# A two-layer fusion block on one core: the last stage's kept norm two images ahead, its sums one image ahead, and the constants loaded after the first image

## The chip, the cores and the metric

The kernel runs on one core of a Trainium2 chip. The metric is the device time of one execution in microseconds (us). Times of events are us from the start of the profiled span. PE is TensorE, DVE is VectorE, ACT is ScalarE, POOL is GpSimd, and SP is SyncE, which here only issues DMAs.

## What is computed

32 images are cut into 196 patches each and projected to 128 columns; 77 text rows are put behind them, so an image has 273 rows. Then come an attention block with mixed heads and a mixture of experts, each added to its input. The tail of the reference is what the last stage computes:

```
h = h + _L0_attn_ref(_layernorm(h, axis=-1), ...)
h = h + _L0_ffn_ref(_layernorm(h, axis=-1), ...)

def _L0_ffn_ref(x, ...):
    xn = layer_norm(x, ln_g, ln_b)
    logits = jnp.einsum('bsd,de->bse', xn, Wg)
    ...                                        # top 2 of 8 experts, two matrices each
    combined = jnp.einsum('bskd,bsk->bsd', sel, conf)
    return layer_norm(x + combined, out_g, out_b)
```

So for each image the end is: y = norm(h), t = y + (the two chosen experts' results), out = h + norm(t) * out_g + out_b.

## The kernel before

There are three stages. The attention stage goes image by image, with nine turns (one for each of eight heads, and one for the last rows) per image, and overlaps three images. It writes h of each image to DRAM (`h1`), keeps the mean and scale of the second norm in SBUF (`kept`), and scatters the normalised rows to the experts' regions in DRAM. The expert stage takes 76 tiles of 256 rows, and scatters the weighted results back to DRAM, two choices for each row. The final stage goes through the 32 images once more. There is no scheduler: the order on each engine is the order in which the code is written.

**How the final stage is ordered.** `slots(eng, total, stages, ring)` walks through steps s on one engine. `stages` is a list of pairs (a, function); in step s the functions run in the listed order, each for image s + a. So a = 2 means that an engine does this part two steps before the image's own step. Each engine has its own list, and engines meet only through semaphores. Of every buffer there are eight, one for each image modulo 8 (`UE`); of the PSUM banks there are four for each of two uses. The parts of image k are:

- SP, `load_image` (six steps ahead): three DMAs, the two expert results (two DMAs, lines 416 and 418) and h (line 419, into a part of `w1hl`); from image 8 on they wait for the output of image k - 8. `store` (two steps behind): two DMAs, lines 423 and 425.
- ACT, `normed3` (line 839): y from h with the kept scale and bias, three activations of 98x128, into `Y3` (a part of `w2s`, so that profile rows call it `w2s`). It waits for the load (`in`) and for a copy of the kept values (`nr3`).
- PE, `sums` (line 1450): the two experts' results are added by two matmuls with the identity. It waits for the load and for the PSUM bank of image k - 4 (`t3`).
- DVE, `sum3` (line 1163): t = sums + y, into `T3` (profile rows call it `w1hl`). Then `stats3`: bn_stats (line 876, three), a small copy (879), bn_aggr (881, three) into `mv3`.
- POOL, `norm3` (lines 651 to 656): four tiny operations that make scale and bias of the third norm.
- ACT, `scale3` (line 847): t times scale plus bias, three activations, in place. It waits for POOL's last one.
- DVE, `scale3` (line 1173): times out_g, in place, both operands in SBUF. It waits for ACT's `scale3`.
- PE, `kept_rows` (line 1458): h + out_b in PSUM; it waits for the output of image k - 4 (`fin`).
- DVE, `output` (line 1182): the sum, into `fin` (profile rows call it `VP`).

DVE also copies the kept values (`stats_back`, line 1156). On DVE the order in step s is stats_back, scale3 of image s - 2, sum3 of s, output of s - 2, stats3 of s.

**How the kernel starts.** SP issues in turn the token weights `wtok` (384 KB), image 0 (588 KB), its text rows (38.5 KB), `wqkv` (320 KB), `cosT` (294 KB), image 1 (588 KB) and its text rows. ACT issues at the same time the bias of the experts (4 KB, line 662) and `small` (1297 KB, line 663), which holds all small constants; it then waits for image 0 (`x0`) and issues the experts' weights (lines 666 to 668, 4 MB). PE's token matmuls of image 0 (line 1201) wait for `wtok` and image 0. DVE waits for `small` before four short preparations (lines 867 to 871), and then adds the token bias, which lies in `small`, to PE's result (line 890).

Of the kernel before, what the change touches and what calls it, by code (L numbers as in the profile page):

```python
# [25 lines left out]
B, C, IMG, P16 = 32, 3, 224, 16  # L26
# [31 lines left out]
UE = 8  # L58
# [28 lines left out]
def early_fusion_kernel(nc, x, txt, w_tok, w_qkvr, small_in, w1, b2, w2, rope, tail, tiota,  # L87
# [5 lines left out]
    with ctx:  # L93
# [3 lines left out]
        def sem(name):  # L97
            return ctx.enter_context(nc.semaphore(name))
# [156 lines left out]
        S = {n: sem(n) for n in names.split()}  # L255
# [46 lines left out]
        def slots(eng, total, stages, by_expert=(), ring=UP):  # L302

            ahead = [a for a, _ in stages]

            def expert(t):
                return eng.value_load(tab[0:1, 0, bass.ds(t, 1)], min_val=0, max_val=NE - 1)

            def peeled(s):
                for a, stage_ in stages:
                    if 0 <= s + a < total:
                        stage_(s + a, (s + a) % ring, *([expert(s + a)] if stage_ in by_expert else []))
            for s in range(-max(ahead), 2 * ring):
                peeled(s)


            halves = []
            for h in range(2):  # L320
                need = {u + a for a, stage_ in stages if stage_ in by_expert for u in (2 * h, 2 * h + 1)}
                if need:
                    first, count = min(need), max(need) - min(need) + 1
                    regs = [eng.alloc_register(f"expert{h}{n}") for n in range(count)]
                    halves.append((first, regs, {first + n: bass.RuntimeValue.of_register_unchecked(
                        r, min_val=0, max_val=NE - 1) for n, r in enumerate(regs)}))

            def load_experts(h, s):
                if halves:
                    first, regs, _ = halves[h]  # L330
                    eng.reg_load(regs, tab[0:1, 0, bass.ds(s + first, len(regs))])
            load_experts(0, 2 * ring)
            with eng.Fori(2 * ring, total - 2 * ring + 1, ring) as s:
                for u in range(ring):
                    if u == 0:
                        load_experts(1, s)
                    if u == 2:
                        load_experts(0, s + ring)
                    for a, stage_ in stages:
                        stage_(s + (u + a), (u + a) % ring,  # L340
                               *([halves[u // 2][2][u + a]] if stage_ in by_expert else []))
            for s in range(total - ring, total - min(ahead)):
                peeled(s)
# [3 lines left out]
        def _(sp):  # L347
# [22 lines left out]
            def step(i, par, has):  # L370
# [6 lines left out]
                if has["load"]:  # L377
# [4 lines left out]
            sp.wait_ge(S["w2_loaded"], 48)  # L382
            sp.wait_ge(S["ends_ready"], 1)
            _, ends = nc.values_load_multi_w_load_instructions(basu[0:1, :], engines=[sp.engine], min_val=0,
                                                               max_val=DUMMY - TT)
            for row in [*ends, DUMMY]:
# [273 lines left out]
        @block.scalar  # L660
        def _(act):
            act.dma_start(bias[:], b2).then_inc(S["bias_in"], 16)
            act.dma_start(small[:], small_in).then_inc(S["small_weights"], 16)
            act.wait_ge(S["x0"], 16)
            for a in range(2):
                act.dma_start(stage[:, a, :], w1[:, a * 2048:(a + 1) * 2048]).then_inc(S["w1_loaded"], 16)
            for dst, src in ((w2s, w2), (tio, tiota), (tailt, tail)):
# [175 lines left out]
            def scale3(k, p):  # L843
# [3 lines left out]
                    last = nc.scalar.activation(T3[p][:, t], T3[p][:, t], ACT.Identity, bias=nm3[:, p, t:t + 1],  # L847
                                                scale=rs3[:, p, t:t + 1])
                last.then_inc(S["c3"], 1)
            slots(act, B, [(0, normed3), (-1, scale3)], ring=UE)  # L850


        @block.vector
        def _(dve):
# [321 lines left out]
            def output(k, p):  # L1176

                dve.wait_ge(S["res_ps"], k + 1)
                if not below(k, UE):
# [1 line left out]
                dve.wait_ge(S["g3"], k + 1)  # L1181
                v.tensor_tensor(fin[p], T3[p], PS[0:R, 4 + p % 4, 0:w].rearrange("p (t d) -> p t d", t=NT), ALU.add
                                ).then_inc(S["fin"], 1)
            slots(dve, B, [(3, stats_back), (-2, scale3), (0, sum3), (-2, output), (0, stats3)], ring=UE)


        @block.tensor
        def _(pe):
# [264 lines left out]
            def kept_rows(k, p):  # L1453
                if below(k, 1):
                    pe.wait_ge(S["bias_row"], 16 * UE)
                if not below(k, 4):
                    pe.wait_ge(S["fin"], k - 3)
                mm(PS[0:R, 4 + p % 4, 0:w].rearrange("p (t d) -> p t d", t=NT), sumb[:], H3b[p], start=True, stop=True
                   ).then_inc(S["res_ps"], 1)
            slots(pe, B, [(0, sums), (-1, kept_rows)], ring=UE)  # L1460


# [83 lines left out]
```

## Time and profile before

| | |
|---|---|
| median of 3 runs | 1436.22 us (1434.65 to 1436.59) |
| the profiled execution's own time | 1437.18 us |
| its span | 1435.3 us |
| PE busy / ACT / DVE / POOL | 92% / 71% / 62% / 58% of the span |
| attention stage | to about 1035 us |
| expert stage | about 1035 to 1315 us |
| final stage, first load issued / first sum / end | 1320.5 / 1327.5 / 1435.3 us |

How to read it: over the whole span PE is the busiest engine, but the figure is a mean over stages. In the final stage no engine is busy all the time, and the last stage is about 8% of the span. There, the chain of waits (which work released which, followed back from the end) says more than busy shares. A row of the timeline shows start, duration, engine, line, operation, output and inputs, how many were merged, and in brackets the idle time before it with what ended it.

### The profile page before, as it was taken

To read this page: it belongs to the slowest core of one execution; us is meant where nothing else is said; L and a number is where in the kernel's file an instruction comes from. 1 tells how busy PE (TensorE), PEld (TensorE's weight loads), DVE (VectorE), ACT (ScalarE), POOL (GpSimd) and SP (SyncE) were. 2 spreads that over 40 slices of the span, in tenths; PEclk is the share of its full clock that TensorE was granted. 3 is DMA by queue.
4 is the path that set the end of the run, shared out by engine and by line. 5 is a ranking of instruction groups with operands and counts; after the bars stand their busy time and mean duration, and the time that the engine had idled before them with its cause. 6 is when DMAs were issued, how large, how long until landed. Compare 5 with 4: busy or idle time off the path is not lost.

```text
span 1435.3 us, 34511 instructions
## 1 busy us (share of the span) xinstructions
PE 1317.1 (92%) x8386; PEld 1099.1 (77%) x8387; DVE 894.0 (62%) x3124; ACT 1024.7 (71%) x3008; POOL 837.9 (58%) x1845
## 2 busy tenths in 40 slices
PE   5899999999999999999999999997699999997874
PEld 4777788777887777787778877776599999996331
DVE  3776666776666766667666667664355444443777
ACT  2688887888888888878888888887155555553676
POOL 2136665566665566655666655666556666665444
PEclk9999999999999999999999999999599999998987
DMA  6001111111110101110111101100222222222763
GB/s 238 19 28 32 37 51 35 31 35 31 50 38 31 35 31 34 50 35 31 35 31 50 38 31 35 31 15 28 72 70 78 77 77 77 75 73 61 198 178 95
DMA packets 69507, 82.39 MB, mean 57 GB/s; under 512 B 11650, under 2 KB 59773, under 8 KB 68946
## 3 DMA queue, kind: packets, MB, share of 16 engines
q1 hardware_dynamic: 57264, 57.17, 13.6%
q0 software_dynamic: 11328, 19.07, 4.3%
q10 hardware_dynamic: 866, 5.60, 0.9%
q8 instruction: 18, 0.29, 0.1%
q14 instruction: 31, 0.25, 0.1%
HBM read 52.13 MB, written 30.65 MB: 58 GB/s over the span
## 4 chain that ended last, share of the span: by engine, by line
PE 55%; DVE 18%; POOL 10%; issue 9%; ACT 5%; DMA 1%; DVEq 1%; ACTq 0%; POOLq 0%; SPq 0%
PE PS L1285 10%; PE PS L1438 10%; PE PS L1247 8%; PE PS L1201 6%; PE PS L1265 4%; DVE bst L876 4%; DVE nmax L954 3%; PE PS L1425 3%; PE PS L1427 3%; PE PS L1426 3%; PE PS L1291 2%; POOL rs L466 2%; ACT E L696 2%; DVE xn L901 2%; POOL qT L489 2%
## 5 line engine op out<-in xcount | busy, mean ns | idle before, releaser
L1247 PE MATMUL PS<-kT,qs 128*128 128x273 f32 x1024 | 281.8, 398 | 1.8 <-ACT E L696 1.4
L1285 PE MATMUL PS<-AT,VP 128*128 128x273 f32 x1024 | 279.4, 395 | 0.0
L696 ACT ACTIVATE E<-PS,nmax 128x273 f32<-128x273 f32 x512 | 243.9, 484 | 25.7 <-DVE nmax L954 21.1
L954 DVE TENSOR_REDUCE nmax<-PS 128x2 f32<-128x546 f32 (+1 forms) x288 | 206.8, 718 | 72.3 <-PE PS L1247 72.3
L585 POOL DMA_INDIRECT dram_routed<-xr,slu x192 | 189.0, 984 | 60.5 <-issue 60.5
L1247 PEld LDWEIGHTS PS<-kT,qs 128*128 128x128 f32 x1024 | 184.4, 190 | 36.2 <-issue 2.9
L641 POOL DMA_INDIRECT dram_results<-arena,du x152 | 166.0, 1092 | 62.9 <-issue 53.3
L723 ACT COPY AT<-PS 128x512 f32<-128x512 f32 x256 | 150.1, 586 | 60.7 <-PE PS L1265 60.7
L1285 PEld LDWEIGHTS PS<-AT,VP 128*128 128x128 f32 x1024 | 175.5, 191 | 20.6
L1265 PEld LDWEIGHTS PS<-small,E 128*128 128x128 f32 x1024 | 126.2, 141 | 53.1 <-ACT ATR L730 22.0
L1265 PE MATMUL PS<-small,E 128*128 128x128 f32 x1024 | 156.4, 274 | 8.9 <-ACT ATR L730 8.7
L1438 PE MATMUL PS<-w2s,VP 128*128 x1216 | 156.3, 278 | 0.0
L1438 PEld LDWEIGHTS PS<-w2s,VP 128*128 128x128 f32 x1216 | 148.4, 192 | 0.0
L679 ACT ACTIVATE qs<-qT,small 128x256 f32<-128x256 f32 x256 | 128.5, 503 | 24.3 <-POOL qT L489 24.3
L933 DVE RECIPROCAL rsum<-esum 128x2 f32<-128x2 f32 (+1 forms) x288 | 45.4, 157 | 160.0 <-ACT E L696 143.0
L826 ACT ACTIVATE VP<-PS,b1f 128x256 f32<-128x256 f32 x304 | 119.3, 474 | 31.8 <-PE PS L1427 31.8
L709 ACT ACTIVATE E<-E,rsum 128x256 f32<-128x256 f32 x256 | 132.7, 518 | 8.7 <-DVE rsum L933 5.0
L505 POOL TENSOR_TENSOR EK<-E,rsum 128x34 f32<-128x34 f32 x256 | 63.1, 253 | 90.9 <-DVE rsum L933 89.0
L817 ACT CAST rounded<-PS 128x256 fp32r<-128x256 f32 x76 | 28.3, 372 | 119.5 <-PE PS L1413 119.5
L939 DVE TENSOR_SCALAR E<-E,rsum 128x256 f32<-128x256 f32 x256 | 101.7, 397 | 9.0
L1201 PE MATMUL PS<-wtok,arena 128*98 128x128 f32 x768 | 98.6, 280 | 9.2 <-DMA arena<-in_x 9.0
L696 ACT ACTIVATION_READ_ACCUMULATOR E<-PS,nmax 128x1 f32 x512 | 102.7, 200 | 0.0
(191 smaller groups left out, 2790.4 us busy)
## 6 DMA issues: line engine op xcount, KB each, us to landing
arena<-in_x SPq DMA_DIRECT2D x32, 588.0 KB
arena<-dram_routed SPq DMA_DIRECT2D x76, 144.0 KB
dram_h<-H SPq DMA_DIRECT2D x32, 147.0 KB
w1hl<-dram_h SPq DMA_DIRECT2D x32, 147.0 KB
stage<-dram_results SPq DMA_DIRECT2D x16, 196.0 KB
AT<-dram_results SPq DMA_DIRECT2D x16, 196.0 KB
out<-VP SPq DMA_DIRECT2D x32, 98.0 KB
dram_routed<-xr,slu POOLq DMA_INDIRECT x192, 2.3
```

The costliest lines, as they stand in the source:

```text
L585: g_.indirect_dma_start(out=routed, out_offset=bass.IndirectOffsetOnAxis(ap=slu[0:rows, par, k, t:t + 1], axis=0), in_=xr[0:rows, par, t, ...
L641: g_.indirect_dma_start(out=results.rearrange("n (k d) -> (n k) d", k=2), out_offset=bass.IndirectOffsetOnAxis(ap=du[:, u, h, :], axis=0), ...
L679: nc.scalar.activation(qs[:, g % QR, :], qT[:, par, 0:MQ], ACT.Copy, scale=wpre[:, g:g + 1]).then_inc(S["q_scaled"], 1)
L696: nc.scalar.activation(bank, PS[0:rows, 2 * ((par + u) % 2) + t, 0:N], ACT.Exp, bias=nmax[0:rows, u, t:t + 1], accum_out=esum[0:rows, u, t ...
L709: last = nc.scalar.activation(own_tile, own_tile, ACT.Copy, scale=rsum[:, u, 1:2])
L723: nc.scalar.copy(AT[:, u - 1, :, 0:MQ], PS[:, TB, :].rearrange("p (c q) -> p c q", c=FULL)).then_inc(S["probsT_sb"], 1)
L954: v.tensor_reduce(nmax[0:rows, u], PS[0:rows, b0:b0 + 2, 0:N], AX.X, ALU.max, negate=True).then_inc(S["max"], 1)
L1201: last = mm(PS[0:R, MA, t * D:(t + 1) * D], xt[:, p, q, t * R:(t + 1) * R], wtok[:, q, :], start=(q == 0), stop=(q == QP - 1))
L1247: last = mm(PS[0:rows, 2 * ((par + u) % 2) + t, 0:N], q, kT[:, par, 0:N], start=True, stop=True)
L1265: last = tr(PS[:, TB, at:at + 128], E[:, (u - 1) % EB, t, keys], idn[:])
L1285: last = mm(acc, VP[:, par, g, c, :], AT[:, g, c, :], start=(g == 0 and c == 0), stop=False)
L1438: mm(o, GT[:, u % 2, c, h * 128:(h + 1) * 128], w2s[:, bass.ds(e * FH + c * D, D)], start=(c == 0), stop=False)
```

## The change

Three numbers and the place of one wait differ. In the final stage ACT's `normed3` runs two images ahead instead of in the image's own step, and PE's `sums` one image ahead. The copy of the kept values, which `normed3` needs, goes from three to four ahead on DVE. At the start ACT's wait for image 0 stands ahead of the DMA of `small` instead of behind it.

```diff
@@ -660,8 +660,8 @@
             act.dma_start(bias[:], b2).then_inc(S["bias_in"], 16)
+            act.wait_ge(S["x0"], 16)
             act.dma_start(small[:], small_in).then_inc(S["small_weights"], 16)
-            act.wait_ge(S["x0"], 16)
             for a in range(2):
@@ -847,7 +847,7 @@
-            slots(act, B, [(0, normed3), (-1, scale3)], ring=UE)
+            slots(act, B, [(2, normed3), (-1, scale3)], ring=UE)
@@ -1181,7 +1181,7 @@
-            slots(dve, B, [(3, stats_back), (-2, scale3), (0, sum3), (-2, output), (0, stats3)], ring=UE)
+            slots(dve, B, [(4, stats_back), (-2, scale3), (0, sum3), (-2, output), (0, stats3)], ring=UE)
@@ -1457,7 +1457,7 @@
-            slots(pe, B, [(0, sums), (-1, kept_rows)], ring=UE)
+            slots(pe, B, [(1, sums), (-1, kept_rows)], ring=UE)
```

What stands in a row on ACT at the start of the kernel, before; names are destination and source, and brackets show what an instruction waits for.

```order
L662 DMA bias<-in_b 128x8
L663 DMA small<-in_small 128x2594
L666 DMA stage<-in_w 128x2048 [waits x0]
L666 DMA stage<-in_w 128x2048
L668 DMA w2s<-in_w 128x4096
```

After the change ACT has there:

```order
L662 DMA bias<-in_b 128x8
L664 DMA small<-in_small 128x2594 [waits x0]
L666 DMA stage<-in_w 128x2048 x2
L668 DMA w2s<-in_w 128x4096
L668 DMA tio<-in_tiota 1x152
```

The wait for image 0 moved from the first expert weights to `small`, which stands ahead of them.

ACT at the start of the final stage (L839 is `normed3`, L847 `scale3`, three activations for an image), as one piece of the difference:

```order
 L826 ISA
 L826 ACTIVATE VP<-PS,b1f 128x256
-L839 ACTIVATE w2s<-w1hl,nr 98x128 x6
+L839 ACTIVATE w2s<-w1hl,nr 98x128 x12
 L847 ACTIVATE w1hl<-w1hl,nm,rs 98x128 x3
 L839 ACTIVATE w2s<-w1hl,nr 98x128 x3
```

Ahead of the first `scale3` there were two images of `normed3`, and now there are four; from there on the two alternate as before, and at the end four images of `scale3` stand in a row instead of two.

PE at the start of the final stage, before (L1450 is `sums`, two matmuls for an image, L1458 `kept_rows`):

```order
L1440 MATMUL PS<-b2hl,ones 128x128
L1450 MATMUL PS<-stage,small 98x384 x4
L1458 MATMUL PS<-w1hl,small 98x384
L1450 MATMUL PS<-stage,small 98x384 x2
L1458 MATMUL PS<-w1hl,small 98x384
L1450 MATMUL PS<-stage,small 98x384 x2
```

After the change PE has there:

```order
L1440 MATMUL PS<-b2hl,ones 128x128
L1450 MATMUL PS<-stage,small 98x384 x6
L1458 MATMUL PS<-w1hl,small 98x384
L1450 MATMUL PS<-stage,small 98x384 x2
L1458 MATMUL PS<-w1hl,small 98x384
L1450 MATMUL PS<-AT,small 98x384 x2
```

The first `kept_rows` stood behind the sums of two images, and now stands behind those of three.

## Rows read from the trace of the kernel before

**Rows 1.** Windows, final stage: length, PE, PEld, DVE, ACT, POOL busy, clock, DMA, GB/s.

```profile
1332.00:1420.00 88.00, 67.77 (x175) 29.54 (x173) 67.82 (x297) 65.03 (x166) 41.00 (x107) 0.92 0.61 171
```

**Rows 2.** Chain of waits, one turn of the final stage: start, us, what.

```profile
1363.35 0.04 ACT w1hl L847
...
1364.61 1.17 ACT w2s L839 x3
...
1365.87 0.09 DVE w1hl L1163
...
1367.66 0.23 DVE mv L881 x3
...
1367.96 0.49 POOL nm L651
...
1369.84 0.05 ACT w1hl L847
```

**Rows 3.** Timeline of the same stretch: start, us, engine, line.

```profile
1361.36 0.55 DVE L1173 TENSOR_TENSOR w1hl<-w1hl,small 98x384 f32<-98x384 f32 x1
1361.47 0.49 POOL L651 TENSOR_TENSOR nm<-mv,mone 98x3 f32<-98x3 f32 x1 [2.50 <-DVE mv L881]
...
1363.35 1.26 ACT L847 ACTIVATE w1hl<-w1hl,nm,rs 98x128 f32<-98x128 f32 x3 [1.77 <-POOL nm L656]
...
1363.53 0.30 DVE L881 BATCH_NORM_AGGREGATE mv<-bst 98x2 f32<-98x6 f32 x3
...
1363.92 0.20 POOL L651 TENSOR_TENSOR nm<-mv,mone 98x3 f32<-98x3 f32 x1 [0.60 <-DVE mv L881]
...
1364.64 0.56 DVE L1173 TENSOR_TENSOR w1hl<-w1hl,small 98x384 f32<-98x384 f32 x1 [0.75 <-ACT w1hl L847]
...
1365.67 1.25 ACT L847 ACTIVATE w1hl<-w1hl,nm,rs 98x128 f32<-98x128 f32 x3
```

**Rows 4.** Timeline, DVE's line 1173 for images 0, 28 and 31.

```profile
1332.19 0.56 DVE L1173 TENSOR_TENSOR w1hl<-w1hl,small 98x384 f32<-98x384 f32 x1 [0.78 <-ACT w1hl L847]
...
1422.97 0.56 DVE L1173 TENSOR_TENSOR w1hl<-w1hl,small 98x384 f32<-98x384 f32 x1 [0.80 <-ACT w1hl L847]
...
1431.54 0.56 DVE L1173 TENSOR_TENSOR w1hl<-w1hl,small 98x384 f32<-98x384 f32 x1 [0.90 <-ACT w1hl L847]
```

**Rows 5.** Timeline of ACT, and one stretch of the windows, as the final stage begins.

```profile
1327.00 1.26 ACT L839 ACTIVATE w2s<-w1hl,nr 98x128 f32<-98x128 f32 x3 [1.11 <-DMA w1hl<-dram_h]
1330.89 0.88 ACT L847 ACTIVATE w1hl<-w1hl,nm,rs 98x128 f32<-98x128 f32 x2 [2.63 <-POOL nm L656]
...
1326.00:1332.00 6.00, 6.00 (x15) 2.85 (x14) 3.34 (x18) 2.37 (x6) 1.93 (x7) 0.74 0.95 248
```

**Rows 6.** Timeline of PE's line 1458 for two images running, and that stretch's window.

```profile
1373.43 1.58 PE L1458 MATMUL PS<-w1hl,small 99*98 99x384 f32 x2 [1.86 <-DVE VP L1182]
...
1377.37 1.48 PE L1458 MATMUL PS<-w1hl,small 99*98 99x384 f32 x2
...
1374.00:1378.00 4.00, 4.00 (x7) 1.71 (x6) 3.21 (x17) 2.24 (x7) 2.72 (x7) 0.50 0.73 192
```

**Rows 7.** Timeline and windows, start of the kernel.

```profile
8.78 0.27 DVE L867 CAST trb<-small 98x196 bf16<-98x196 f32 x1 [5.09 <-DMA small<-in_small]
...
9.23 0.17 DVE L871 COPY base<-small 98x8 f32<-98x8 f32 x1
14.51 0.42 DVE L890 TENSOR_TENSOR H<-PS,small 98x256 f32<-98x256 f32 x1 [5.12 <-PE PS L1201]
...
9.03 5.44 PE L1201 MATMUL PS<-wtok,arena 128*98 128x128 f32 x24 [9.03 <-DMA arena<-in_x]
...
2.00:5.00 3.00, 0.00 (x0) 0.00 (x0) 0.34 (x2) 0.00 (x0) 1.99 (x7) 1.00 0.93 368
5.00:9.00 4.00, 0.00 (x0) 0.00 (x0) 0.22 (x2) 0.00 (x0) 0.36 (x1) 1.00 1.03 390
9.00:12.00 3.00, 2.97 (x14) 2.97 (x15) 0.36 (x4) 0.70 (x1) 0.05 (x1) 1.00 1.10 408
```

## The prediction

> **What bounds the kernel now.** I read three views in turn. First the windows, to see whether an engine is full in the stage that the change touches. From 1332 to 1420 us DVE is busy for 67.8 of 88 us, ACT for 65.0, PE for 67.8, and the DMA engines move 171 GB/s at a share of 0.61 [rows 1]: nobody is full, so a chain of waits sets the pace. Then the chain of waits there. It repeats with a period of 1369.84 - 1363.35 = 6.49 us [rows 2], and one turn does two images: on DVE, line 1173 of image 0 starts at 1332.19 and of image 28 at 1422.97, 90.78 us for 28 images, 3.24 us each [rows 4]. One turn is ACT's `scale3`, then ACT's `normed3` of a later image, then DVE's line 1163, which waits for that `normed3`, then output and statistics, POOL's norm, and ACT again. So y, which depends on nothing in the loop, sits in it because ACT takes its work in the order in which it is written. Third the timeline of the start: PE's first matmul waits until 9.03 us for image 0, and `small`, which has landed by 8.78 us, is needed by nobody on the path before line 890 at 14.51 us [rows 7].
>
> **The final stage, term by term.** The present turn, from the rows: from ACT's line 847 to the start of DVE's line 1163, 1365.87 - 1363.35 = 2.52 us; from there to the end of the last bn_aggr, 1367.66 + 0.23 - 1365.87 = 2.02; from there through POOL to ACT's next line 847, 1369.84 - 1367.89 = 1.95. Sum 6.49 [rows 2].
>
> With `normed3` two ahead, y of image k is finished before ACT begins `scale3` of image k - 3, so line 1163 no longer waits for ACT's second job. What is late next is DVE's line 1173 of image k, which still wants `scale3` of k, and stands ahead of the sum and statistics of image k + 2 on DVE. The new turn: ACT's line 847 to DVE's line 1173, 1364.64 - 1363.35 = 1.29 us; line 1173 to the end of bn_aggr where DVE waited for nothing, 1363.53 + 0.30 - 1361.36 = 2.47; through POOL to ACT, 1.95 as now [rows 2, 3]. Sum 5.71 us for two images, 0.78 less than 6.49.
>
> Does something else take over above 5.71? For two images: DVE's own work by the timeline is two of the 2.47 us stretches, 4.94. ACT, densely packed, needs 1365.67 - 1363.35 = 2.32 us for an image [rows 3], 4.64. PE at the low clock needs 1377.37 - 1373.43 = 3.94 us for one image back to back with a granted clock of 0.50 [rows 6]; at full clock half of that, my estimate, 3.94 for two. An image moves 556 KB (loads 420, stores 136), 0.57 MB; at the 248 GB/s that the stage reached with the DMA engines at 0.95 [rows 5] that is 2.30 us, 4.6 for two. All are below 5.71, so the loop remains the bound, and DVE will be busy for about 86% of it.
>
> Edits with no cost of their own: the kept copy on DVE one image earlier lies in DVE's wait for the first loads; PE already runs some four images ahead of DVE, as its banks allow, so that sums one image earlier neither help nor hurt in the middle. SP's order is the same; its five DMAs for an image follow DVE's outputs and get no new wait.
>
> **One term in it is a question of contention.** POOL's line 651 took 0.49 us when it began 0.11 us after DVE's line 1173, and ended as that did; begun with DVE idle it took 0.20 [rows 3]. In the new turn DVE again goes straight from one image's statistics into line 1173 of another, in every second image, and the slower of the two sets the loop; so I keep 1.95. Without it the turn would be 5.71 - 0.29 = 5.42. The Trainium skill (SBUF — State Buffer, section "Who interferes with whom") says that a DVE operation with two inputs in SBUF makes a GpSimd operation that reads SBUF wait until it is through; the trace agrees, with 0.49 against 0.20 us. By that rule the turn is 5.71, by a mere scatter of POOL's durations it would be 5.42.
>
> **Head and tail of the stage.** At the head the edit costs something: ACT now has four `normed3` ahead of the first `scale3`, so `scale3` of image 0 stands behind the load of image 3. Images 0 and 1 had landed by 1327.0 at the latest [rows 5]; at 0.43 MB an image and 248 GB/s each further one takes 1.75 us, so image 3 lands about 1330.5. With `normed3` of it, 1.2 us (1.17 in rows 2), `scale3` of image 0 starts at 1331.7 to 1332.1 instead of 1330.89 [rows 5]: +1.2 us, and up to +3 if the loads come in late. Then 14 turns lead to image 28's line 1173: 1332.19 + 1.2 + 14 x 5.71 = 1413.3 against 1422.97, a gain of 9.6. From there to line 1173 of image 31 it took 8.57 us [rows 4]; the same two steps with the loop's new waits take 5.71 + 2.47 less the shorter POOL time, about 7.9: 0.6 more. The end behind it does not change. Final stage: -10.2 us. Bounds: -8.4 with image 3 at its latest, -14.3 with turns of 5.42.
>
> **The start.** The change gives image 0 the DMA engines for itself. From the windows, 368 GB/s x 3 us + 390 x 4 = 2.66 MB had moved by 9.0 us, when both image 0 and `small` had landed [rows 7]; they, `wtok` and the small pieces are 2.37 MB. Without `small`, 1.04 MB must move; at 368 GB/s from 2.0 us on that is 4.8 us, and with the same overshoot of 0.3 MB 5.6. PE then has 5.44 us of matmuls [rows 7], so it is through at 10.3 to 11.1 instead of 14.5. But line 890 needs `small` as well, which is only issued at about 5. All that SP has queued, `small` and the bias are 3.64 MB; work that keeps the engines full as now has moved them at 9.0 + (3.64 - 2.66) / 0.408 = 11.4 us [rows 7]. After `small` DVE has its four preparations, 9.23 + 0.17 - 8.78 = 0.62 us, so line 890 starts at 12.0 instead of 14.51: -2.5 us. That is the value I take, because the engines were full from 2 to 12 us. Bounds: if `small` had the engines for itself from 4.8 on (8.2 us), PE's 10.3 would decide, -4.2; if the queues ran dry for 2 us, as long as the head of the kernel before the first window of [rows 7], 13.4 + 0.6 = 14.0, -0.5. So a gap in the queues decides whether this part is worth anything. What else waits for `small` has cover: POOL's two preparations are due only when the statistics of line 890's result are done, and the expert weights, which now come behind it, are first used in the fourth turn of image 0. The attention stage has no start time of its own, so the shift passes through to the end.
>
> **Sum.** -10.2 - 2.5 = -12.7 us. The profiled execution took 1437.18 us, so 1424.5; it lies 0.96 us above the median of the runs, which gives 1423.5 for a median.
>
> **Rivals.**
> 1. The clock (slower). PE needs 3.94 us for an image at the low one of its two levels (1.2 of 2.4 GHz; 0.50 granted) [rows 6], more than the 3.24 of now. If the clock stayed low through the stage, PE would be the bound: from 1327.0, where image 1 is in [rows 5], 31 x 3.94 us, and 3.8 from line 1173 of image 31 to the end of the span [rows 4], 1452.9, less 2.5 of the start, which is 1451 as a median. It binds from the point where more than about 45% of the stage is low (1.97 x 1.45 = 2.86), and turns to a loss beyond 65%. Against: the mean granted clock of 1332 to 1420 is 0.92, some 16% of it low [rows 1], PE ran four images ahead meanwhile, and a shorter turn leaves shorter pauses. The skill (TensorE: Matmul & The Clock Gate, section "HAM oscillation — how this bites in real kernels") warns that pauses between bursts bring the low clock back each time; the dips are there, with pauses of 1.86 us ahead of a burst [rows 6], but no wait of DVE shows behind them. 4%.
> 2. The DMA engines. If loads and stores mixed go no faster than the 192 GB/s of [rows 6], an image takes 2.97 us, a turn 5.94: 14 x 0.55 - 1.2 + 0.6 = -7.1, and 1426.6. For it: the share is 0.73 there. Against: 0.95 is reached when more is asked for. 8%.
> 3. Turns of 5.42 without the contention: -14.3, so 1419.4. 8%.
> 4. `small` comes late, the start is worth 0.5 or less: 1425.5 to 1426. 10%.
> 5. It doesn't do what it says: the later y was never the late one, and the wait for `scale3` moves in for the same time. Then only the head's cost and the start remain: 1435. Against it the 2.52 us that lie between line 847 and line 1163, of which 1.17 is `normed3` [rows 2]. 3%.
>
> **How the numbers follow.** The forecast has 67%, with a range of its own of 1421 to 1426. About 0.2% of the time, 3 us, is what a measurement of this kernel can tell from no change. Faster by more: the forecast and rivals 2 to 4, 93%. Within: rival 5, 3%. Slower: rival 1, 4%. The range takes in the bounds of head and start and rivals 2 and 4, and the nearer part of rival 3: 1419.5 to 1428.5.
>
> **What would show it.** In the profile after: line 1163 no longer waits for ACT's line 839, line 1173 waits for ACT's line 847 once in two images, turns of 5.7 us; ACT's first line 847 near 1332 less the shift; PE's first matmul at about 5 us, line 890 released by `small` near 12. Wrong would be turns above 5.9, a wait of ACT for loads past the first four images, or `small` after 13 us.

## The result, and the profile of the changed kernel

The changed kernel took 1424.67 us (median of 6 runs, 1424.06 to 1428.46), the kernel before, on the same chip, 1436.06 us (6 runs): a ratio of 0.9926, with an interval of 0.9913 to 0.9939. The medians differ by 11.4 us (0.8%), and the time lies inside the predicted range, 1.2 us above the predicted value. The profiled execution of the changed kernel took 1424.06 us, with a span of 1422.2 us; it is the fastest of the six.

**The final stage in windows.** Columns as in [rows 1]: stretch, length, PE, PEld, DVE, ACT, POOL busy (instructions), granted clock, DMA share, GB/s.

```profile
1330.00:1405.00 75.00, 60.39 (x173) 26.42 (x171) 63.80 (x285) 61.91 (x159) 40.25 (x105) 1.00 0.68 199
```

DVE is busy for 63.80 of 75 us, 85%, where it was 77% in [rows 1]. The granted clock is 1.00 (2.4 GHz) throughout, where it was 0.92. The DMA engines move 199 GB/s, with room left at a share of 0.68. Still nobody is full, so a chain still sets the pace.

**The chain of waits, one turn** (start, us, what):

```profile
1352.14 0.05 ACT w1hl L847
...
1353.43 0.04 DVE w1hl L1173
1353.47 0.44 issue
1353.91 0.17 DVE w1hl L1163
...
1354.38 0.54 DVE VP L1182
...
1355.70 0.23 DVE mv L881 x2
...
1356.00 0.49 POOL nm L651
...
1356.72 0.86 POOL rs L654
...
1357.88 0.05 ACT w1hl L847
```

From one `scale3` on ACT to the next there are 1357.88 - 1352.14 = 5.74 us for two images, where [rows 2] had 6.49. ACT's line 839, a link of the chain in [rows 2], is gone: y of the image is ready long before, so line 1163 follows line 1173 without a wait for ACT.

**The waits of the stage, 1318 to 1415** (engine, line, what it waited for: us in total, times, longest), four of them:

```profile
ACT w1hl L847 <- POOL nm L656: 14.9, 15, 1.0
...
ACT w2s L839 <- DMA w1hl<-dram_h: 14.3, 4, 12.7
DVE w1hl L1163 <- PE PS L1450: 12.2, 2, 11.8
DVE w1hl L1173 <- ACT w1hl L847: 11.7, 15, 1.0
```

Before, this view (1327 to 1425) also had line 1163 waiting for ACT's line 839, once in two images:

```profile
DVE w1hl L1163 <- ACT w2s L839: 10.0, 15, 0.7
```

That wait is gone. What is left is one wait of line 1173 for ACT in two images, which was there before as well (11.4 us, 15 times), and the 15 waits of ACT for POOL that close the loop.

**Line 1173 for images 0, 28 and 31**, to set beside [rows 4], and POOL's line 651 with line 1173 beside it, to set beside [rows 3] (timeline: start, us, engine, line, and in brackets the idle time before with what ended it):

```profile
1330.50 0.56 DVE L1173 TENSOR_TENSOR w1hl<-w1hl,small 98x384 f32<-98x384 f32 x1 [1.05 <-ACT w1hl L847]
...
1352.71 0.19 POOL L651 TENSOR_TENSOR nm<-mv,mone 98x3 f32<-98x3 f32 x1 [0.61 <-DVE mv L881]
...
1355.88 0.55 DVE L1173 TENSOR_TENSOR w1hl<-w1hl,small 98x384 f32<-98x384 f32 x1
1356.00 0.49 POOL L651 TENSOR_TENSOR nm<-mv,mone 98x3 f32<-98x3 f32 x1 [1.74 <-DVE mv L881]
...
1410.68 0.56 DVE L1173 TENSOR_TENSOR w1hl<-w1hl,small 98x384 f32<-98x384 f32 x1 [0.80 <-ACT w1hl L847]
...
1418.49 0.56 DVE L1173 TENSOR_TENSOR w1hl<-w1hl,small 98x384 f32<-98x384 f32 x1 [0.90 <-ACT w1hl L847]
```

14 turns take 1410.68 - 1330.50 = 80.18 us, 5.73 each, where they took 90.78. From image 28 to 31 it is 7.81 us, where it was 8.57. In every second image line 651 begins 0.12 us behind line 1173 and takes 0.49 us; in the others it takes 0.19.

**ACT at the head of the stage**, to set beside [rows 5], with SP's first load issue of the stage:

```profile
1318.41 0.38 SPq L416 DMA_DIRECT2D stage<-dram_results  x1
...
1322.75 1.26 ACT L839 ACTIVATE w2s<-w1hl,nr 98x128 f32<-98x128 f32 x3 [12.74 <-DMA w1hl<-dram_h]
1324.40 1.26 ACT L839 ACTIVATE w2s<-w1hl,nr 98x128 f32<-98x128 f32 x3 [0.39 <-DMA w1hl<-dram_h]
...
1328.06 1.26 ACT L839 ACTIVATE w2s<-w1hl,nr 98x128 f32<-98x128 f32 x3 [0.54 <-DMA w1hl<-dram_h]
1329.22 1.25 ACT L847 ACTIVATE w1hl<-w1hl,nm,rs 98x128 f32<-98x128 f32 x3
```

Four images of line 839 wait for their loads (the 4 waits of the list above), the first image lands at 1322.75, the second at 1324.40, the fourth at 1328.06. Only then does `scale3` of image 0 come, with no wait of its own.

**The start**, to set beside [rows 7] (timeline, then windows):

```profile
5.70 0.34 ACTq L664 DMA_DIRECT2D small<-in_small  x1
5.72 4.71 PE L1201 MATMUL PS<-wtok,arena 128*98 128x128 f32 x24 [5.72 <-DMA arena<-in_x]
12.56 0.26 DVE L867 CAST trb<-small 98x196 bf16<-98x196 f32 x1 [8.56 <-DMA small<-in_small]
13.09 0.41 DVE L890 TENSOR_TENSOR H<-PS,small 98x256 f32<-98x256 f32 x1
```

```profile
2.00:5.00 3.00, 0.00 (x0) 0.00 (x0) 0.34 (x2) 0.00 (x0) 1.68 (x6) 1.00 0.94 349
5.00:6.00 1.00, 0.28 (x1) 0.28 (x2) 0.00 (x0) 0.00 (x0) 0.67 (x2) 1.00 0.92 287
6.00:9.00 3.00, 3.00 (x15) 3.00 (x15) 0.00 (x0) 0.49 (x1) 0.00 (x0) 1.00 1.15 396
9.00:12.00 3.00, 1.44 (x11) 1.22 (x9) 0.00 (x0) 0.79 (x1) 0.00 (x0) 1.00 1.00 411
```

Image 0 is in at 5.72 instead of 9.03, and PE is through at 10.4. But `small` comes at 12.56, and line 890 starts at 13.09 instead of 14.51: 1.42 us earlier.

**Where the time went.** The stage from SP's first load issue to the end of the span took 1435.3 - 1320.50 = 114.8 us before and 1422.2 - 1318.41 = 103.8 us after: -11.0 us. All that lies ahead of it ended 2.09 us earlier in this pair of profiled executions. How much of these 2.09 us the change made is a question for the experiments, since the attention and expert stages do not take the same time in every execution.

### The profile page after: what moved, and what is told of

The parts are those of the page before. It is cut to its first block, busy times and chain, and to the rows that moved or that the text cites. A ratio compares the mean times of both kernels' runs of the same rounds, so it can differ in the third digit from the quotient of the medians.

```text
span 1422.2 us, 34511 instructions
## 1 busy us (share of the span) xinstructions
PE 1309.2 (92%) x8386; PEld 1095.2 (77%) x8387; DVE 891.8 (63%) x3124; ACT 1025.0 (72%) x3008; POOL 837.8 (59%) x1845
## 4 chain that ended last, share of the span: by engine, by line
PE 56%; DVE 18%; POOL 9%; issue 9%; ACT 4%; DMA 1%; DVEq 1%; ACTq 0%; POOLq 0%; SPq 0%
PE PS L1285 10%; PE PS L1438 10%; PE PS L1247 8%; PE PS L1201 6%; PE PS L1265 4%; DVE bst L876 4%; DVE nmax L954 3%; PE PS L1425 3%; PE PS L1427 3%; PE PS L1426 3%; PE PS L1291 2%; POOL rs L466 2%; ACT E L696 2%; DVE xn L901 2%; POOL qT L489 2%
## 5 line engine op out<-in xcount | busy, mean ns | idle before, releaser
L939 DVE TENSOR_SCALAR E<-E,rsum 128x256 f32<-128x256 f32 x256 | 101.6, 397 | 9.0
```

## The experiments

All kernels here compute the whole of the reference. Diffs are against the changed kernel, unless the text says otherwise. "Stage" is the time from SP's first load issue of the final stage to the end of the span, "turn" the time from one `scale3` on ACT to the next but one, both from each kernel's own profile. The ratio is against the kernel before, with its interval.

| kernel | median us | ratio | line 890, image 0 | first load of the stage | stage | turn |
|---|---|---|---|---|---|---|
| before | 1436.06 | 1 | 14.51 | 1320.50 | 114.8 | 6.49 |
| changed | 1424.67 | 0.9926 [0.9913, 0.9939] | 13.09 | 1318.41 | 103.8 | 5.74 |
| e1 start alone | 1435.65 | 0.9997 [0.9988, 1.0007] | 13.16 | 1319.36 | 115.1 | 6.49 |
| e2 final stage alone | 1424.11 | 0.9920 [0.9904, 0.9937] | 14.35 | 1319.21 | 103.6 | 5.74 |
| e3 norm one ahead | 1424.00 | 0.9921 [0.9904, 0.9937] | 13.12 | 1318.58 | 102.9 | 5.72 |
| e4 sums in step | 1424.52 | 0.9923 [0.9906, 0.9939] | 13.51 | 1320.00 | 104.2 | 5.73 |
| e5 gain in PSUM | 1421.48 | 0.9899 [0.9882, 0.9915] | 14.18 | 1318.31 | 101.6 | 5.50 |
| e6 lag of three | 1409.42 | 0.9819 [0.9798, 0.9840] | 13.58 | 1318.68 | 89.8 | 4.88 |
| e7 weights behind `small` | 1422.39 | 0.9905 [0.9889, 0.9922] | 13.37 | 1319.64 | 103.9 | 5.73 |
| e8 `small` issued by SP | 1422.74 | 0.9912 [0.9895, 0.9928] | 11.26 | 1315.47 | 104.3 | 5.73 |
| e9 e6 and e8 together | 1407.55 | 0.9813 [0.9800, 0.9827] | 11.04 | 1315.87 | 89.8 | 4.88 |
| e10 e6 with the start of before | 1411.92 | 0.9831 [0.9818, 0.9845] | 14.60 | 1320.34 | 90.1 | 4.88 |
| e11 e6 and e5 together | 1410.99 | 0.9831 [0.9816, 0.9847] | 13.41 | 1320.35 | 90.1 | 4.87 |

### e1 and e2: the two halves of the change apart

e1 is the kernel before with the moved wait at the start alone; e2 has the lists of the final stage alone (against the changed kernel):

```diff
             act.dma_start(bias[:], b2).then_inc(S["bias_in"], 16)
-            act.wait_ge(S["x0"], 16)
             act.dma_start(small[:], small_in).then_inc(S["small_weights"], 16)
+            act.wait_ge(S["x0"], 16)
```

> The kernel before with one edit, ACT's wait for image 0 ahead of the DMA of the constants; the final stage as before. Theory (the two parts add up): line 890 of image 0 near 13.1 us instead of 14.5, the first load of the final stage about 2 us earlier, and the final stage's own length unchanged at 114.8 us: a ratio of 0.9985, 1434.0 us. Rival (the 2 us at the end of the expert stage come from elsewhere, such as a run's scatter): line 890 earlier, but the time within 0.5 us of the kernel before.

> The three changed numbers of the final stage, the start as before. Theory: turns of 5.73 us for two images instead of 6.49, the stage 11.0 us shorter, line 890 at 14.5: a ratio of 0.9923, 1425 to 1425.5 us. Rival (part of the gain of the stage hangs on the earlier start): less than 10 us.

Measured: e1 1435.65 us, -0.4 us against before with an interval from -1.7 to +1.0; e2 1424.11 us, no slower than the whole change. So the final stage carries all of the gain that can be measured. In e1 line 890 does start 1.35 us earlier (13.16), and its final stage is the same within 0.3 us. The interval leaves open whether these 1.35 us reach the end or nothing does; the 2.1 us of its theory lie outside it.

The profiles of ten kernels say why that is hard to read. The first load of the stage was issued at 1320.50, 1319.21 and 1320.34 us with the old start (before, e2, e10; mean 1320.0), and at 1318.41, 1319.36, 1318.58, 1320.00, 1318.31, 1318.68 and 1320.35 with the changed one (changed, e1, e3 to e6, e11; mean 1319.1). The means differ by 0.9 us, the single values by 2. From line 890 to that load lie between 1304.1 (e5) and 1306.9 us (e11), and the first windows show what varies there (kernel before, then changed, then e2; columns as above):

```profile
36.00:52.00 16.00, 11.91 (x48) 8.96 (x47) 15.30 (x30) 9.21 (x30) 3.07 (x8) 0.79 0.00 1
```

```profile
36.00:52.00 16.00, 12.48 (x53) 9.76 (x52) 14.22 (x30) 9.36 (x30) 3.19 (x8) 0.79 0.00 1
```

```profile
36.00:52.00 16.00, 10.72 (x56) 7.89 (x55) 14.94 (x30) 9.67 (x31) 3.19 (x8) 1.00 0.01 2
```

The granted clock, third from the end of the row, is 0.79 in two of them and 1.00 in e2, whose line 890 started late and whose first load is 1.3 us earlier than that of before all the same. Nearly all of the difference arises at the front. From line 890 of image 3 (at 99.08 us before) to that load it takes 1221.2 to 1221.8 us in every one of the thirteen profiles; from line 890 of image 0 to that of image 3 it takes between 82.9 and 85.6 us. The granted clock goes with it: in the eight profiles with 0.79 from 36 to 52 us these three images take 84.1 us or more, in the five with 0.89 or 1.00 they take 82.9 to 83.6. So the phases of TensorE's clock in the first images go with differences as large as what the start is worth. That the clock is their cause is not shown by a run of its own, and what makes it high in one execution and low in another stays open. What is left of the changed start is -0.9 us by the means, with no interval that excludes zero; with the clock alike it is -1.1 us (0.79: before and e10 against changed, e1, e3, e4 and e11) and -0.5 us (1.00: e2 against e6).

### e3 and e4: how far ahead

e3 runs `normed3` one image ahead instead of two, e4 runs `sums` in the image's own step.

```diff
-            slots(act, B, [(2, normed3), (-1, scale3)], ring=UE)
+            slots(act, B, [(1, normed3), (-1, scale3)], ring=UE)
```

```diff
-            slots(pe, B, [(1, sums), (-1, kept_rows)], ring=UE)
+            slots(pe, B, [(0, sums), (-1, kept_rows)], ring=UE)
```

> The changed kernel with ScalarE's norm one image ahead instead of two. Theory (what counts is only that y is ready before ACT takes the scale of an image two back, so a lead of one is enough): turns of 5.73 us as with two, the first line 847 behind the load of image 2 instead of image 3, which takes back up to 0.4 us; 1424.2 to 1424.8 us. Rival (two are needed, since the norm then stands just behind a scale that waits for POOL): turns between 5.73 and 6.49, up to 1435 us.

> The changed kernel with PE's sums back in the image's own step. Theory (PE ran some four images ahead of DVE anyway, so this part is worth nothing): turns of 5.73 us, the same time within 0.5 us, 1424.7. Rival (with faster turns PE's sums become the late ones): turns above 5.9 us and line 1163 waiting for PE.

Measured: 1424.00 and 1424.52 us, turns of 5.72 and 5.73. One image of lead for y is enough. In e3 the head of the stage is shorter, because `scale3` of image 0 has three images of line 839 ahead of it, not four (timeline of ACT):

```profile
1326.33 1.26 ACT L839 ACTIVATE w2s<-w1hl,nr 98x128 f32<-98x128 f32 x3 [0.49 <-DMA w1hl<-dram_h]
1328.55 1.26 ACT L847 ACTIVATE w1hl<-w1hl,nm,rs 98x128 f32<-98x128 f32 x3 [0.96 <-POOL nm L656]
```

It starts 1328.55 - 1318.58 = 9.97 us after the first load issue, against 1329.22 - 1318.41 = 10.81 in the changed kernel, and it now waits for POOL, not for ACT's own queue: 0.8 us of the head are the second image of lead, where 0.4 were expected, and the stage is 0.9 us shorter. In e4 the waits of line 1163 for PE between 1330 and 1405 come to 0.2 us in all. The lead of `sums` is worth nothing here.

### e5: POOL's line 651 without the neighbour

`out_g` is copied once into free columns of PSUM, so that line 1173 (here line 1177) reads one operand from SBUF and one from PSUM. It then also has to wait for PE's `kept_rows` of that image, which lie in the same bank. (The name of the new semaphore is left out here.)

```diff
+            v.tensor_copy(PS[0:R, 4:8, w:w + D], outg[:].unsqueeze(1).broadcast_to([R, 4, D])
+                          ).then_inc(S["gain_ps"], 1)
...
+                dve.wait_ge(S["res_ps"], k + 1)
                 dve.wait_ge(S["c3"], k + 1)
-                v.tensor_tensor(T3[p], T3[p], outg[:].unsqueeze(1).broadcast_to([R, NT, D]), ALU.mult
-                                ).then_inc(S["g3"], 1)
+                v.tensor_tensor(T3[p], T3[p], PS[0:R, 4 + p % 4, w:w + D].unsqueeze(1).broadcast_to([R, NT, D]),
+                                ALU.mult).then_inc(S["g3"], 1)
...
+                    pe.wait_ge(S["gain_ps"], 1)
```

> The changed kernel with out_g copied once into free columns of the four PSUM banks that the outputs use, so that DVE's line for the gain (1173 in the changed kernel) has one operand in SBUF and one in PSUM. Theory (POOL's first operation of the norm is held back by a DVE operation with both operands in SBUF): that POOL operation takes 0.20 us in every image instead of 0.49 in every second, turns of 5.42 to 5.45 us instead of 5.73, 14 turns of 0.29 us: 4 us off, 1420.6 us. Rival (POOL's 0.49 us has another cause, such as its own scatter or any DVE work): still 0.49, turns of 5.73, 1424.7.

Measured: 1421.48 us, where the theory had 1420.6, and a stage 2.2 us shorter. The chain of waits, one turn:

```profile
1357.20 0.05 ACT w1hl L847
...
1358.49 0.02 DVEq L1176
...
1358.56 0.06 DVE w1hl L1177
...
1361.12 0.19 POOL nm L651
...
1362.70 0.05 ACT w1hl L847
```

Line 651 takes 0.19 us in every image, and the turn is 5.50 us. Of the 0.29 us that left line 651, 0.07 came back: from ACT's line 847 to DVE's multiplication it is 1.36 us, where it was 1.29; the second wait of that instruction (line 1176) now stands in the chain ahead of it. The same wait costs at the head: line 1177 of image 0 starts 1331.03 - 1318.31 = 12.72 us after the first load issue, held by PE's `kept_rows`, where it was 12.09. That is why 14 turns gave 3.1 us and the stage only 2.2. Line 1177 still runs beside line 651 (it starts at 1361.02), so it is not any work of DVE that held POOL back: the 0.49 us were contention with line 1173 and its second operand in SBUF, not scatter. The rule that the prediction cited from the Trainium skill (SBUF — State Buffer, section "Who interferes with whom") agrees: 0.49 us with two operands in SBUF, 0.19 with one.

### e6 and e11: a longer lag, and whether the two gains add

e6 puts DVE's `scale3` and `output` three steps behind instead of two, and changes nothing else. e11 has e5's edit on top of it.

```diff
-            slots(dve, B, [(4, stats_back), (-2, scale3), (0, sum3), (-2, output), (0, stats3)], ring=UE)
+            slots(dve, B, [(4, stats_back), (-3, scale3), (0, sum3), (-3, output), (0, stats3)], ring=UE)
```

> The changed kernel with DVE's gain and output three images behind instead of two. Theory (the loop from statistics through POOL and ACT back to DVE is what is left, and DVE has no other wait): the loop is spread over three images, 5.71 / 3 = 1.9 us, so DVE's own 2.47 us an image sets the pace: turns of 4.95 us for two images instead of 5.73, 14 turns of 0.78, and one more image's output in the tail, +0.5 to +1: 10 us off, 1414.5 us. Rival (the DMA engines: 0.57 MB an image in 2.47 us is 231 GB/s, near the 250 that the stage has reached): turns of 5.3 us or more with ACT or PE waiting for loads, 1419 or later.

> The lag of three images of e6, with the gain read from PSUM as in e5, so that line 1173's successor (line 1177) no longer reads two operands from SBUF. Theory, GpSimd's hold-back lies in a loop that no longer binds (VectorE's own work does): line 651 falls from 0.49 to 0.20 us in every image, the turns stay at 4.88 us and the time at 1409.4 us, give or take 0.5. Rival, the gains add: turns shorter by about 0.2 us, 15 of them, 1406.5 us.

Measured: e6 1409.42 us, a stage 14.0 us shorter than in the changed kernel, and 5 us better than the 1414.5 expected. Line 1173 starts at 1331.04 for image 0, at 1399.11 for image 28 and at 1404.74 for image 31. So 14 turns take 68.07 us, 12.1 less than in the changed kernel, where 10.9 were expected, and the way from image 28 to 31 takes 5.63 us, 2.2 less, where the longer lag was expected to cost 0.5 to 1. The rival, the DMA engines, did not come: they moved the 235 GB/s that the pace needs (below). The chain in e6 is DVE alone:

```profile
1355.54 0.46 DVE w1hl L1173
1356.00 0.09 DVE w1hl L1163
1356.09 0.30 issue
1356.38 0.54 DVE VP L1182
1356.92 0.60 DVE bst L876 x3
...
1357.62 0.30 DVE mv L881 x3
1357.92 0.05 DVE nr L1156
1357.98 0.46 DVE w1hl L1173
```

An image takes 1357.98 - 1355.54 = 2.44 us, and no other engine stands in it. The windows of e6 from 1340 to 1380:

```profile
1340.00:1380.00 40.00, 35.99 (x104) 15.77 (x103) 39.41 (x185) 39.72 (x101) 27.31 (x67) 1.00 0.79 235
```

DVE is busy for 39.41 of 40 us; ACT is nearly full beside it, though its first two `scale3` of the stage stand 2.31 us apart, so ACT could go a little faster. Now the stage is bound by work, not by a loop. In e6 line 651 still takes 0.49 us, and now in every image. In e11 it is short again (DVE's line 1177 and POOL's line 651, timeline):

```profile
1352.42 0.55 DVE L1177 TENSOR_TENSOR w1hl<-w1hl,PS 98x384 f32<-98x384 f32 x1
1352.54 0.19 POOL L651 TENSOR_TENSOR nm<-mv,mone 98x3 f32<-98x3 f32 x1 [0.88 <-DVE mv L881]
...
1357.29 0.55 DVE L1177 TENSOR_TENSOR w1hl<-w1hl,PS 98x384 f32<-98x384 f32 x1
```

Two images take 1357.29 - 1352.42 = 4.87 us, as in e6. e11's time, 1410.99 us, is no better than e6's, though it lies above the 1409.4 give or take 0.5 of its theory; its stage is 0.3 us longer than that of e6, the rest lies ahead of the stage (first load at 1320.35). The 2 to 3 us that the same edit was worth in e5 are gone, because POOL's hold-back no longer lies on the path that binds.

### e7, e8, e9 and e10: the start

e7 makes ACT wait for `small` before the experts' weights, to learn whether these overtake it. e8 gives `small` to SP, right behind image 0 and its text rows. e9 is e8's start with e6's lag, e10 the start of before with e6's lag.

```diff
@@ e7
             act.dma_start(small[:], small_in).then_inc(S["small_weights"], 16)
+            act.wait_ge(S["small_weights"], 16)
@@ e8
             load_txt(0)
+            sp.dma_start(small[:], small_in).then_inc(S["small_weights"], 16)
             sp.dma_start(wqkv[:], w_qkvr).then_inc(S["qkv_weights"], 16)
...
-            act.wait_ge(S["x0"], 16)
-            act.dma_start(small[:], small_in).then_inc(S["small_weights"], 16)
+            act.wait_ge(S["small_weights"], 16)
```

> The changed kernel with a second wait on ACT, for the constants, ahead of the DMAs of the experts' weights. Theory (some 0.3 MB of the weights queued behind the constants on ACT's queue moved before the constants were complete): the constants land 0.7 us earlier, line 867 at 11.8 instead of 12.56 us, and the kernel is 0.7 us faster, 1424.0. Rival (the constants are late because the engines were slower from 5 to 6 us, or by their own queue): line 867 still at 12.3 to 12.6 us.

> The changed kernel with the constants issued by SP right behind image 0 and its text rows, and ACT waiting for them ahead of the experts' weights. Theory (the two queues share the engines, so that the constants, issued at 5.7 us, wait for what SP has queued; in one queue they come in turn, 2.37 MB at 370 to 390 GB/s): image 0 lands near 5.7 us, the constants near 8.5 to 9, line 890 follows PE's last token matmul at about 10.5 us instead of 13.1: 2.5 us off, 1422.2 us. Rival (one queue alone does not keep the engines full, or completions of one queue wait for each other): line 890 at 12 us or later, image 0 later than 6.5 us.

In e7 `small` was seen on DVE at 12.84 us, no earlier than in the changed kernel, so the weights that come behind it were not what delayed it. Its windows:

```profile
5.00:6.00 1.00, 0.29 (x1) 0.30 (x2) 0.00 (x0) 0.00 (x0) 0.47 (x1) 1.00 0.93 273
6.00:9.00 3.00, 3.00 (x15) 3.00 (x15) 0.00 (x0) 0.00 (x0) 0.00 (x0) 1.00 1.15 380
9.00:12.00 3.00, 2.14 (x11) 1.80 (x9) 0.00 (x0) 0.00 (x0) 0.00 (x0) 1.00 0.91 374
12.00:13.00 1.00, 0.00 (x0) 0.00 (x0) 0.16 (x1) 0.00 (x0) 0.68 (x2) 1.00 0.05 21
```

From 12 us on only 21 KB move, and none after 12.2: the bytes are there by then, and the engine that waits for them starts at 12.84. So 0.6 to 0.8 us lie between the last bytes and the waiting instruction. e7's time, 1422.39 us, has an interval that overlaps the changed kernel's. In e8 image 0 was seen at 6.74 instead of the 5.7 expected, `small` at 10.09, later than the 8.5 to 9 expected, and line 890 started at 11.26, 1.8 us earlier than in the changed kernel. The time, 1422.74 us, has an interval that overlaps the changed kernel's.

> The lag of three images of e6 together with the start of e8 (small constants issued by SyncE right behind image 0). Theory, the two parts are independent and add: line 890 of image 0 at about 11.3 us, turns of two images 4.88 us, time 1409.4 - 1.9 = 1407.5 us. Rival, what the start gains is lost again in the clock's phases of the first two images: 1409.4 us, with line 890 at 11.3 us all the same and the first load of the final stage no earlier than in e6 (1318.7 us).

> The lag of three images with the start of the kernel before (ScalarE waits for image 0 alone, so the constants come as they did there). Theory, the changed start is worth about 1 us at line 890: line 890 at 14.4 us and a time of 1410.4 us. Rival, it is worth nothing that reaches the end: 1409.4 us.

Measured: e9 1407.55 us, as its theory said, with the first load of the stage at 1315.87 us, 2.8 us ahead of e6's 1318.68. e8's was at 1315.47: these two lie outside the 1318.3 to 1320.4 of all other changed starts, so with `small` on SP the gain does reach the final stage. e10, 1411.92 us, is above what either side expected (1410.4 or 1409.4); against e9, on the same chip, the two starts are 4.4 us apart by the medians, 3.56 of which line 890 shows (14.60 to 11.04). The size is uncertain: single executions go from 1409.22 to 1412.81 us in e10 and from 1407.14 to 1410.43 in e9, the means are 3.0 us apart, and the intervals of the two ratios overlap. e11, with the changed start, lies between them at 1410.99. e9 beats both kernels: 0.9813 of the kernel before.

## Why the prediction was right, point by point

- **The loop and its new turn: right.** 5.71 us for two images were predicted from three pieces, 5.73 are the mean of 14 turns. The pieces came out too: from ACT to line 1173 1353.43 - 1352.14 = 1.29 us; on DVE to the end of bn_aggr 1355.70 + 0.23 - 1353.43 = 2.50, where 2.47 were predicted; through POOL to ACT, with the long line 651, 1357.88 - 1355.93 = 1.95. Line 1163 no longer waits for ACT. What was called late next, line 1173 waiting for `scale3`, is what the list of waits shows, 15 times.
- **The contention term: right**, and e5 shows the cause, not only its size: without the second operand in SBUF the turn is 5.50 us, where the prediction's rival 3 had 5.42. Of the 0.08 between, 0.07 lie where e5's extra wait stands.
- **The head: mis-sized, +0.4 us where +1.2 were predicted.** Line 1173 of image 0 starts 1330.50 - 1318.41 = 12.09 us after the first load issue, before 1332.19 - 1320.50 = 11.69. The step took 1327.0 as the landing of images 0 and 1 "at the latest" and added two loads of 1.75 us to get 1330.5, that is 10.0 us after the issue; image 3 landed after 9.65 us (1328.06), because image 1 came 5.99 us after the issue (1324.40), not 6.50 as before. The rest is the choice within the prediction's own working: it gave 1331.7 to 1332.1 for `scale3`, 0.8 to 1.2 later than before, and the sum took the upper end. Measured, `scale3` starts 10.81 us after the issue, where it was 1330.89 - 1320.50 = 10.39. The spacing of the loads, 1.75 us, was right: three of them took 1328.06 - 1322.75 = 5.31 us, 1.77 each.
- **The tail: right.** 7.81 us from image 28 to 31, 7.9 predicted. With the head, the final stage gave -11.0 us where -10.2 were predicted.
- **The start: right in sign, too large.** -2.5 us were predicted at line 890; -1.42 came in the profile of the changed kernel, and that is an early one: in the seven profiles with this start (e7 aside) line 890 starts at 13.09 to 14.18 us, mean 13.44, in the three with the old start at 14.35 to 14.60, mean 14.49. In e5 and e6 `small` was seen after 13 us (13.66 and 13.05), which the prediction had named as a sign of being wrong. What is left at the end is about -0.9 us by the means of the profiles, not told from zero by e1. The step that failed is "work that keeps the engines full as now has moved them at ... 11.4 us". Two things are missing in it. First, until `small` was issued the engines were slower than before: 349 instead of 368 GB/s from 2 to 5 us, and 287 instead of 414 from 5 to 6, so that 1.047 + 0.287 + 1.188 = 2.52 MB have moved by 9.0 us and not 2.66, worth 0.14 / 0.41 = 0.3 us. Second, the overshoot: before, 2.66 MB had moved when 2.37 MB were seen as landed. The prediction put these 0.3 MB into the landing of image 0 but left them out of the landing of `small`, where they are worth 0.29 / 0.41 = 0.7 us, about the 0.6 to 0.8 us that e7's windows show between the last bytes and the instruction. 11.4 + 0.3 + 0.7 = 12.4; measured 12.56.
- **That the start passes through to the end** was the second weak step. It said that "the attention stage has no start time of its own"; the way from line 890 to the final stage varies by 2.8 us between profiles, nearly all of it in the first three images, where the granted clock varies too. From there on a shift does pass through, within 0.6 us.
- **Rivals.** The low clock of rival 1 did not come: the granted clock is 1.00 from 1330 to 1405. Rival 2, engines that go no faster than 192 GB/s, is refuted by 199 GB/s at a share of 0.68 here and 235 GB/s in e6. Rival 3, turns of 5.42, did not come: 5.73. Rival 4, a start worth 0.5 us or less, is not excluded: e1 allows it. Rival 5, nothing but the head's cost, is refuted by a stage that is 11.0 us shorter.
- **The sum.** -12.7 us were predicted against the profiled execution, 1424.5; that of the changed kernel took 1424.06. Against the medians -11.4 us came: -11.0 of the stage, and the rest within the scatter of the start. The two mis-sized terms, 0.8 too much at the head and 1.1 to 1.6 too much at the start, had opposite signs, and the profiled execution began its final stage 2.09 us earlier, of which the change accounts for about 0.9. So the loop, which is 10.6 of the 11.0 us, was predicted well; that the sum came out within 0.5 us of that execution is in part luck.

## What to carry to other kernels

Where engines take their work in written order, count the loop through all of them: a step taken out of it (here y on ACT) gains only the wait that it ended, 0.76 us in a turn, and the loop remains the bound. To lift the bound, give the loop more lag: three steps instead of two between DVE's statistics and DVE's use of them, one number in two places, gave 14 us more, until DVE's own 2.44 us an image were the limit. And before taking a hold-back away, look whether it lies on the path that binds: the same 0.29 us were worth 2 to 3 us in one order (e5) and nothing in the other (e11).

## What was not expected of the hardware

- In the window from 5 to 6 us the DMA engines moved 287 (changed) and 273 GB/s (e7), and with the constants on SP 256 (e9) and 190 (e8); with the start of before they moved 414. All of them are at 346 to 368 GB/s from 2 to 5 us. Why one microsecond is so much poorer was not settled; in all four ACT's queue had nothing to move then, or had only just been given `small`.
- The first load scatters: with the same start ACT saw image 0, and issued `small`, at 5.45 us in e11 and at 7.27 us in e5. A DMA that waits for another one takes over its scatter.
- A multiplication of 98x384 with its second operand in PSUM took 0.55 us, as with both in SBUF.
- ACT and DVE, both over 98% busy in e6, did not slow each other: line 847 took 482 ns an activation there and 481 before, line 1163 550 and 554 ns.
